# Layer norm constants for two groups at once, eight pieces of x, and the candidate product in another stage

## The reference

```python
x = _layernorm(x + _L0_gnn_ref(x, edge_index, ...))            # two GCN layers, degrees under a root
x = _layernorm(x + _L1_gnn_ref(x, ..., src, dst))              # three SAGE layers
x = _layernorm(x + _L2_gnn_ref(x, edge_index, ...))            # gated recurrent unit over attention messages
x = _layernorm(x + _L3_gnn_ref(x, edge_index, ...))            # neighbours' sum and self
# inside _L2: what the change touches
i_r, i_z, i_n = jnp.split(aggregated @ W_ih.T + b_ih, 3, axis=1)
h_r, h_z, h_n = jnp.split(x @ W_hh.T + b_hh, 3, axis=1)
n = jnp.tanh(i_n + r * h_n)                                    # the candidate
h_new = (1.0 - z) * n + z * x                                  # then batch norm over the nodes
# _layernorm: (x - mean) / sqrt(var + 1e-5) over the 128 features
```

## Time and profile before

| what | us |
|---|---|
| median of 3 runs | 5639.57 (5635.73 to 5640.15) |
| the profiled execution's own time | 5636.52 |
| its span | 5634.7 |
| PE busy | 4777.9 (85%) |
| DVE busy | 3858.3 (68%) |
| POOL busy | 2987.3 (53%) |
| ACT busy | 2724.4 (48%) |

### The profile page before, as it was taken

The page is one execution under the profiler, slowest core; times in us unless marked ns, Lnnn a source line. Parts: engine busy times, 40 slices in busy tenths (PEclk is TensorE's granted clock), DMA queues, the critical chain, the costliest instruction groups (busy, mean ns, idle before and its releaser), DMA issues. The chain is left out here.

```text
span 5634.7 us, 104476 instructions
## 1 busy us (share of the span) xinstructions
PE 4777.9 (85%) x27497; PEld 3774.6 (67%) x27497; DVE 3858.3 (68%) x11909; ACT 2724.4 (48%) x6602; POOL 2987.3 (53%) x2962
## 2 busy tenths in 40 slices
PE   4399996666799989999999997888799999447887
PEld 4378885555688867777777775777566666226887
DVE  8467775776688855555555554888677777786676
ACT  2644444655333322222222223776666666794555
POOL 0077765777677743333333325777455554006776
PEclk5599997778899989999999998999899999558999
DMA  3879994555677754444444443877555554794554
GB/s 118 283 228 276 273 273 145 150 148 147 182 240 239 235 167 150 152 149 152 150 152 149 152 141 102 205 198 200 187 170 162 165 170 140 238 306 131 153 149 140
DMA packets 522952, 1023.82 MB, mean 182 GB/s; under 512 B 107859, under 2 KB 115066, under 8 KB 519738
## 3 DMA queue, kind: packets, MB, share of 16 engines
q1 hardware_dynamic: 422970, 803.07, 43.3%
q0 software_dynamic: 99840, 219.14, 16.4%
HBM read 686.55 MB, written 335.29 MB: 181 GB/s over the span
## 5 line engine op out<-in xcount | busy, mean ns | idle before, releaser
L840 POOL DMA_INDIRECT s_rows<-t_h,s_index x416 | 525.2, 1263 | 831.4 <-DVE s_index L833 730.3
L840 POOL DMA_INDIRECT cb_rows<-t_x,cb_index x416 | 396.0, 952 | 456.9 <-DVE cb_index L833 333.5
L840 POOL DMA_INDIRECT g_rows<-t_x,g_index x416 | 415.8, 1000 | 414.8 <-issue 385.1
L840 POOL DMA_INDIRECT at_rows<-t_m,at_index x416 | 423.5, 1018 | 381.9 <-DVE at_index L833 277.3
L840 POOL DMA_INDIRECT s_rows<-t_v,s_index x416 | 400.9, 964 | 211.4 <-issue 123.4
L840 POOL DMA_INDIRECT s_rows<-t_x,s_index x416 | 416.9, 1002 | 152.8 <-issue 117.3
L840 POOL DMA_INDIRECT g_rows<-t_h,g_index x416 | 402.8, 968 | 171.9 <-issue 123.1
L904 PE MATMUL bank<-s_onehot,s_hi 128*128 128x80 f32 (+9 forms) x1758 | 438.1, 289 | 42.4 <-DVE s_lo L875 26.6
L1723 DVE TENSOR_TENSOR s_rout<-bank,s_x 128x512 f32<-128x512 f32 x98 | 67.8, 692 | 586.9 <-PE bank L1667 586.9
L904 PE MATMUL bank<-g_onehot,g_rows 128*128 128x80 f32 (+9 forms) x1172 | 297.7, 418 | 198.5 <-DMA g_rows<-t_h,g_index 178.0
L904 PE MATMUL bank<-s_onehot,s_lo 128*128 128x80 f32 (+9 forms) x1758 | 432.2, 286 | 0.0
(11 more groups left out here) (333 smaller groups left out, 12990.5 us busy)
## 6 DMA issues: line engine op xcount, KB each, us to landing
s_scale<-inv_d SPq DMA_DIRECT2D x196, 256.0 KB
t_h<-s_hout SPq DMA_DIRECT2D x98, 512.0 KB
s_own<-t_h SPq DMA_DIRECT2D x98, 512.0 KB
t_m<-s_mout SPq DMA_DIRECT2D x98, 264.0 KB
at_own<-t_m SPq DMA_DIRECT2D x98, 264.0 KB
t_x<-so_x SPq DMA_DIRECT2D x98, 256.0 KB, 4.3
g_own<-t_x SPq DMA_DIRECT2D x98, 256.0 KB
g_scale<-dinv_d SPq DMA_DIRECT2D x98, 256.0 KB
```

Source lines behind the costliest of these rows:

```text
L840: pool.indirect_dma_start(out=self.rows[:, self.ring(q) + k, :], out_offset=None, in_=self.table[0:NPAD, :], in_offset=bass.IndirectOffset ...
```

## The change

Four edits:

1. `PIECES` has eight pieces in place of five, with `ROOT_AT` for them. `LAST_ROUND` becomes 3, 7, 12, 18, 25, 32, 41, 48, and pieces are inverted 3 or 4 rounds after their last round in place of 3 or 5.
2. `PairedLayerNorm` takes the place of `LayerNorm` in sage_third and batch_normed. The statistics instruction leaves, per block, mean and variance sum of even and odd elements; the new class does not aggregate each block, it combines the halves of two groups (8 blocks) with five small VectorE instructions, and root, reciprocal and shift come once for two groups, on the odd group's turn.
3. The lags change with it: in sage_third `apply` 8 to 9, `turn` 9 to 10, `hold` 10 to 11, `message` 11 to 12, `bias` 12 to 13; in batch_normed ScalarE's `apply` 3 to 4, VectorE's `invert` 2 to 3, and its place on VectorE is now between `add` and `gauge`.
4. The product of x with the candidate's part of W_hh leaves `gates` in attend. `message` in sage_third makes it, ScalarE copies it out (`note`), SyncE stores it to a new DRAM tensor hxt (256 KB per group) and attend loads it (`hx`); `blend` reads it from SBUF. The turned x has one PSUM bank in place of two.

```diff
-PIECES = ((0, 6), (6, 22), (22, 42), (42, 64), (64, T))
+PIECES = ((0, 6), (6, 14), (14, 24), (24, 36), (36, 50), (50, 64), (64, 82), (82, T))
-ROOT_AT = (None, 5, 13, 26, 55)
+ROOT_AT = (None, 5, 13, 23, 34, 47, 61, 76)
...
-                        if n == LAST_ROUND[i] + (3 if i == 0 else 5):
+                        if n == LAST_ROUND[i] + (3 if i < 3 else 4):
                             invert_roots(i)
...
+    class PairedLayerNorm:
+        def take_stats(self, dve, q, z):
+            for b in range(BLK):
+                last = dve.bn_stats(self.stats[q.r // 2][:, q.u * BLK + b, :], z[:, b * D:(b + 1) * D])
+            if q.u == 0:
+                return
+            two = q.r // 2
+            last.then_inc(self.link, 1)
+            wait_for(dve, self.link, q.n * 3 + 1)
+            even, odd = self.stats[two][:, :, 1], self.stats[two][:, :, 4]
+            dve.tensor_tensor(self.apart[two][:, :], even, odd, ALU.subtract)
+            dve.tensor_tensor(self.total[two][:, :], even, odd, ALU.add)
+            dve.tensor_tensor(self.spread[two][:, :], self.stats[two][:, :, 2], self.stats[two][:, :, 5], ALU.add)\
+               .then_inc(self.link, 1)
+            dve.wait_ge(self.link, q.n * 3 + 2)
+            dve.tensor_tensor(self.square[two][:, :], self.apart[two][:, :], self.apart[two][:, :], ALU.mult)\
+               .then_inc(self.link, 1)
+            dve.wait_ge(self.link, q.n * 3 + 3)
+            dve.scalar_tensor_tensor(out=self.spread[two][:, :], in0=self.square[two][:, :], scalar=D / 4,
+                                     in1=self.spread[two][:, :], op0=ALU.mult, op1=ALU.add)\
+               .then_inc(self.varied, 1)
+        def root(self, act, q):
+            if q.u == 1:
+                act.wait_ge(self.varied, q.n + 1)
+                act.activation(self.std[q.r // 2][:, :], self.spread[q.r // 2][:, :], ACT.Sqrt,
+                               bias=ln_eps[:, 0:1], scale=1.0 / D).then_inc(self.rooted, 1)
+        def invert(self, dve, q):
+            if q.u == 0:
+                return
+            two = q.r // 2
+            dve.wait_ge(self.rooted, q.n + 1)
...
+            dve.reciprocal(self.rstd[two][:, :], self.std[two][:, :]).then_inc(self.link2, 1)
...
+               .then_inc(self.scaled, 1)
+        def normalise(self, act, q, to, z):
+            act.wait_ge(self.scaled, q.n + 1)
...
@@ sage_third, TensorE @@
+                    if not (isinstance(q.t, int) and q.t < 1):
+                        pe.wait_ge(noted, q.t)
+                    pe.matmul(bank[5][:, :], whh_s[:, 2 * P:3 * P], xt[q.u][:, :], start=True, stop=True)\
+                      .then_inc(hidden, 1)
...
-                over_groups(pe, [(9, turn), (3, flip), (1, sums), (11, message)])
+                over_groups(pe, [(3, flip), (1, sums), (12, message), (10, turn)])
@@ sage_third, ScalarE @@
+                def note(q):
+                    act.wait_ge(hidden, q.t + 1)
...
+                    act.activation(hx[q.u][:, :], bank[5][:, :], ACT.Copy).then_inc(noted, 1)
-                over_groups(act, [(2, catch), (10, hold), (4, weight), (6, lambda q: ln.root(act, q)), (8, apply)])
+                over_groups(act, [(2, catch), (13, note), (11, hold), (4, weight), (6, lambda q: ln.root(act, q)),
+                                  (9, apply)])
@@ attend, SyncE and TensorE @@
+                    load(sp, q, hx[s][:, :], slab_of(hxt, q.t), loaded_h[s], mixed, XS)
...
-                    if not (isinstance(q.t, int) and q.t < 1):
-                        pe.wait_ge(mixed, q.t)
-                    f = slice(2 * P, 3 * P)
-                    pe.matmul(bank[5][:, :], whh_s[:, f], xq[:, :], start=True, stop=True)
-                    pe.matmul(bank[6][:, :], wih_s[:, f], agg[q.u][:, :], start=True, stop=True)\
+                    if not is_first(q.t):
+                        pe.wait_ge(mixed, q.t - 1)
+                    pe.matmul(bank[5 + q.u][:, :], wih_s[:, 2 * P:3 * P], agg[q.u][:, :], start=True, stop=True)\
                       .then_inc(joined, 1)
@@ batch_normed, ScalarE and VectorE @@
-                over_groups(act, [(0, scale), (2, lambda q: ln.root(act, q)), (3, apply)])
+                over_groups(act, [(0, scale), (2, lambda q: ln.root(act, q)), (4, apply)])
...
-                over_groups(dve, [(0, add), (1, gauge), (2, lambda q: ln.invert(dve, q))])
+                over_groups(dve, [(0, add), (3, lambda q: ln.invert(dve, q)), (1, gauge)])
```

More of the change, by code:

```diff
@@ L957, in normalise, with __init__ @@
                                       bias=self.shift[q.u][:, b:b + 1], scale=self.rstd[q.u][:, b:b + 1])
+            last.then_inc(self.applied, 1)
+    class PairedLayerNorm:
+        def __init__(self, ph):
+            self.stats = ph.pair("ln_stats", [P, 2 * BLK, 6])
+            self.total, self.apart, self.square, self.spread, self.std, self.rstd, self.shift = (
+                ph.pair(f"ln_{n}", [P, 2 * BLK])
+                for n in ("total", "apart", "square", "spread", "std", "rstd", "shift"))
+            self.link = ph.sem("ln_link")
+            self.link2 = ph.sem("ln_link2")
+            self.varied = ph.sem("ln_varied")
+            self.rooted = ph.sem("ln_rooted")
+            self.scaled = ph.sem("ln_scaled")
+            self.applied = ph.sem("ln_applied")
+        def take_stats(self, dve, q, z):
[28 more added lines that the diff above has]
+            dve.wait_ge(self.rooted, q.n + 1)
+            if not is_first(q.t, 4):
+                dve.wait_ge(self.applied, q.t - 3)
+            dve.reciprocal(self.rstd[two][:, :], self.std[two][:, :]).then_inc(self.link2, 1)
+            dve.wait_ge(self.link2, q.n + 1)
+            dve.scalar_tensor_tensor(out=self.shift[two][:, :], in0=self.total[two][:, :], scalar=-0.5,
+                                     in1=self.rstd[two][:, :], op0=ALU.mult, op1=ALU.mult)\
+               .then_inc(self.scaled, 1)
+        def normalise(self, act, q, to, z):
+            act.wait_ge(self.scaled, q.n + 1)
+            two = q.r // 2
+            for b in range(BLK):
+                i = q.u * BLK + b
+                last = act.activation(to[:, b * D:(b + 1) * D], z[:, b * D:(b + 1) * D], ACT.Identity,
+                                      bias=self.shift[two][:, i:i + 1], scale=self.rstd[two][:, i:i + 1])
@@ L1755, in sage_third @@
             asks, st_a = ph.pair("asks", [P, BLK]), ph.sems("stored_a")
+            hx, st_h, noted, hidden = ph.pair("hx", [P, GRP]), ph.sems("stored_h"), ph.sem("noted"), ph.sem("hidden")
             block = ctx.enter_context(nc.Block())
@@ L1790, in turn @@
                     pe.wait_ge(ln.applied, q.t + 1)
-                    if not is_first(q.t):
-                        pe.wait_ge(held, q.t - 1)
+                    if not (isinstance(q.t, int) and q.t < 1):
+                        pe.wait_ge(held, q.t)
                     for b in range(BLK):
-                        last = pe.transpose(bank[4 + q.u][:, b * P:(b + 1) * P],
+                        last = pe.transpose(bank[4][:, b * P:(b + 1) * P],
                                             x2[q.u][:, b * D:(b + 1) * D], ident[:, :])
```

55 lines of the change are left out of this document (32 added, 23 removed).

## The result

The changed kernel takes **5577.19 us** (median, 5576.38 to 5580.25), the kernel before in the same session 5638.23 (5635.73 to 5640.15): ratio 0.9893, 95% interval 0.9881 to 0.9905. In a second session it took 5577.03, ratio 0.9895 (0.9878 to 0.9911). The forecast was 5584. The span of the profiled execution falls from 5634.7 to 5575.6 us, by 59.1.

| stage | before | after | after, again | forecast for the change |
|---|---|---|---|---|
| sort_and_scale | 281.7 | 261.8 (-19.9) | 257.5 | -19 |
| gcn_first and gcn_second | 1157.0 | 1157.6 | 1158.7 | 0 |
| sage_first | 570.6 | 576.1 | 575.5 | 0 |
| sage_second | 1414.3 | 1412.7 | 1414.2 | 0 |
| sage_third | 570.9 | 589.3 (+18.4) | 586.4 | +8 |

The account below looks back on a forecast made before the run. Each stage was taken to have its own bound: GpSimd's gathers in sage_third, TensorE in attend, a ScalarE-VectorE chain in batch_normed, scaling in the sort. -19 - 80 + 8 + 37 = -54 gave 5582.5, stated as 5584, range 5545 to 5622.

Parts of the forecast that it names:

- Pieces, -19: Sort_and_scale: with eight pieces fewer groups wait for the last inverse, scaling ends near 250 us; -19 us, bounds -10 and -24.
- Attend, -80: Attend: the candidate's product, 0.86 us a group, leaves TensorE, the only bound; 93 groups counted, -80 us, bounds -40 and -84.
- The ring of ScalarE and VectorE: Attend, rival: gate, blends and tanh take TensorE's place as bound, half the gain goes, 5624 us; chance 0.09.
- the estimate was 26 us: Attend: by the skill's 131 ns per 512-column matmul the product is worth 0.26 us a group; the forecast used the trace instead.
- Batch_normed, +37: Batch_normed: paired norm makes ScalarE wait every second pass, 2.96 us a group against 2.58; +37 us, bounds +30 and +45.
- the step I called 1.99 us: Batch_normed, every second pass: from ScalarE's start of the scale, through VectorE's add and inversion, to `apply`; 1.99 us.
- The rule of highest occupancy: Batch_normed: relieve the busiest engine; ScalarE (0.92) and VectorE (0.89) are both relieved, so by it the no-stall rival happens.
- the rival without the stall: Batch_normed: the stall does not come, 2.4 us a group, -17 us in place of +37, total 5530; chance 0.08.
- Sage_third, +8: Sage_third: added product stays under GpSimd's 5.34 us a group, one more pipeline step; +8 us, bounds 0 and +30.
- the drain: Sage_third's end: pipeline one step deeper, draining steps each have one more product and copy; about +6 us.
- the wait for the single bank: Sage_third, TensorE: it queues `turn`, but needs only ScalarE's work of the pass before or early in the same; no size given.
- The clock rival: Sage_third: TensorE's mean clock falls to 0.75, its row takes 6.4 us and is the bound, about 5682 us; chance 0.05.

Follow-up runs that it names:

- Experiment 4: The changed kernel with the candidate's second product back in attend, without its store and load, paired norms kept: 5649.67 us, ratio 1.0022.
- experiment 1: The changed kernel with VectorE's `invert` ahead of `add` in batch_normed instead of behind it: 5538.66 us, ratio 0.9819.
- experiment 5: The kernel of experiment 1 with sage_third's layer norm done group by group again, moved product and its store kept: 5535.03 us, ratio 0.9815.
- (8): The kernel before with eight pieces, and TensorE's order in sage_third flip, sums, message, turn; two banks, product in attend: 5614.06 us, a single run.
- (10): The kernel of experiment 1 with the DRAM tensor hxt declared behind all others, no instruction different: 5539.13 us, ratio 0.9822.
- (6): The changed kernel with four buffers instead of two, each with its own semaphore, for sage_third's three stored tiles: 5569.06 us, ratio 0.9876.
- experiment 7: TensorE's old order in sage_third (`turn` first), on the kernel of experiment 5: 5556.3 us; on that of experiment 1: 5568.95 us, a single run.
- 7 on top of 5: The kernel of experiment 5 with TensorE's order in sage_third put back to turn, flip, sums, message: 5556.3 us, ratio 0.9852.

## Why the prediction was right, and where its terms were not

Total, sign and each mechanism's sign were right; of the four terms two were off by 10 to 14 us, with opposite signs. So that the total came within 7 us is in part luck: measured minus forecast is -0.9 for the sort, -4.5 for attend, +10.4 for sage_third and -14.4 for batch_normed, and +4.3 for the stages forecast at nothing. The term of batch_normed lies outside its own bounds (+30 to +45).

- **Pieces, -19.** The one profile gave -19.9 and the last scaling at 248.19, where about 250 was forecast. The thirteen profiles with eight pieces lie between 253.7 and 262.2 us, with a mean of 258.8: -20 to -28 against the single profile before, -23 in the mean, with the mean inside the bounds and the five lowest profiles beyond -24. So the hit of the one profile is chance within that spread. What I had not counted is that a stage fed by DMA varies by as much as the terms I was arguing over.
- **Attend, -80.** -84.5, half a us past the bound: 98 x 0.86 = 84.3, all groups counted, not 93. Experiment 4 gives it back whole (828.7). The ring of ScalarE and VectorE stayed under TensorE, though nearer than before: ScalarE waited 54.3 us in the stage for VectorE's blend, 6.8 before, and 108.0 for TensorE's sums, 245.9 before. By the figure of the Trainium skill (TensorE: Matmul & The Clock Gate, Back-to-back issue gap) the estimate was 26 us; the traces of this case do not agree with it, the product's two instructions were worth 0.86 us.
- **Batch_normed, +37.** The mechanism is shown by experiment 1, and the step I called 1.99 us measured 2.00. The mis-sized term is the rest of the pair: I took root to `apply` as 0.36, a distance that in the earlier trace rows contains a wait of 0.16 for the shift, and scale to root as 0.79. That one too contains a wait, for the variance: before, VectorE's last step to it ends at 4934.24 and the root starts at 4934.27.

```profile
4934.07 0.17 DVE L936 TENSOR_SCALAR bn_ln_var<-bn_ln_mv 128x4 f32<-128x4 f32 x1
```

In the changed kernel the second pass has variance and shift already, and the distances are 0.70 and 0.19. 2.00 + 1.39 + 0.70 + 0.19 + 1.37 = 5.65 in place of 5.92, a difference of 0.27 a pair, 13 of the 14 us. The root on 8 columns lasts 0.30 us (0.20 on 4), but the next instruction starts 0.19 after it, so its length did not count.
- **The rule of highest occupancy** (the Trainium skill, Perfetto Trace Analysis, Identifying the Most-Contended Engine). Both engines at the top were relieved, to 0.80 and 0.70 of the time, and the stage took 285.8 us in place of 263.2: the traces of this case do not agree with the rule where two engines wait for each other in a fixed order. With the order put right (experiment 1) the same instructions give 250.3, less than before; the rival without the stall had 263 - 17 = 246.
- **Sage_third, +8.** +18.4 and +15.5, inside the bounds. The 5 us between first and last gather come with the paired norm alone (experiment 4) and with the product alone (experiment 5), not with the order (8), the place of hxt (10) or too few buffers (6); a gather took 976 ns in the mean against 964, 416 x 0.012 = 5.0 (977 and 978 in experiments 4 and 5, 966 in 8). Which resource lengthens it stays open; the DMA share, forecast at 0.93, was 0.87 in the window above. The mis-sized term is mainly the drain, the time behind the last gather: +9.3 to +13.4 in place of 6. The paired norm's pass more is worth 6.0 there by itself (experiment 4) and the product with its copy and store 6.4 (experiment 5); I had counted 6 for both. In this part I also wrote that the wait for the single bank needs only what ScalarE did earlier. That holds for the order of the changed kernel; experiment 7 shows that it rests on `turn` standing last, some 27 us that I had not priced.
- **The clock rival** did not come: with TensorE busy 183.70 of 200 us in place of 163.10 the granted clock was 0.98 in place of 0.94, in the whole stage 0.93 in place of 0.90.

## What to carry to other kernels

When a step is moved in a list that an engine works off in order, write down one period of both engines from start to start, and ask of each distance whether it contains a wait that the change removes. Halving small instructions is worth nothing while their result comes one wait late: here one swap in a list was worth 35.5 us, where the right order with all the saved instructions gained 12.9 against the kernel before. Where a buffer is given up (two banks to one), look at the order of the steps again. And with work that is done once for two groups, moving a lag by one changes which pass, the long or the short one, stands ahead of the consumer. Last, a total that fits does not confirm its terms: measure them one by one.

## What the runs showed of the hardware, unexpected

In the profile before, TensorE's granted clock was 0.50 in the sort from 40 us on, the lower of its two levels (1.2 GHz); in the one after it was 1.00, the higher (2.4 GHz). The short bf16 matmuls took the same time at both. TensorE, 90 to 190 us, before and after (busy us, mean ns):

```profile
L498 PE MATMUL bank<-so_count,so_parts 128*128 128x16 bf16 (+1 forms) x667 | 84.9, 208 | 0.0
```

```profile
L500 PE MATMUL bank<-so_count,so_parts 128*128 128x16 bf16 (+1 forms) x642 | 81.6, 209 | 0.0
```

Most of these have 16 columns: 208 and 209 ns. They overlap; all of TensorE's instructions there come to 1371 in 87.58 us of busy time before and 1327 in 87.04 after, 64 and 66 ns each.

The level is not the change's doing. Of the thirteen profiles with eight pieces ten ran this window at 1.00 and three at 0.50 (experiments 4, 7 on top of 5, and 10), with the same work ahead of it: TensorE was busy 12.3 to 12.4 of the 50 us from 40 to 90 at either level. The sorts of the three took 260.6, 261.4 and 255.9 us, those of the ten 253.7 to 262.2. So the clock explains neither the gain of the eight pieces nor the spread of the sort. What decides the level in an execution is open.

And sage_first, whose instructions the change leaves alone, took 570.6 to 580.2 us in the profiles of this case, a spread as large as some of the terms in question. A difference within that spread between single profiles of that stage is not a finding. The readings of sage_third rest on more: its time from first to last gather was 525.8 to 527.2 us in the three profiles without paired norm and moved product, and 530.8 to 538.0 in the eleven with either.
